# Three output projections, each in one stage with the layer norm that follows it

## The reference, cut to what matters

```
x = x + attn(norm(x));   attn ends in  out @ w_proj + b_proj + 2 * (out @ la @ lb)     (16 heads, causal)
x = x + xattn(norm(x));  xattn ends in out @ Wo + bo        (8 heads of 64, so out has 512 channels)
x = x + routed(norm(x)); routed ends in O @ Wo + bo         (4 of 16 heads of 64, chosen from the mean of norm(x))
x = x + attn2(norm(x)) ...
norm(x) = (x - mean) / sqrt(var + 1e-5), over the 256 channels, without gain or bias
```

## Time and profile before

| what | value |
|---|---|
| median of 3 runs | 2760.14 us (2759.46 to 2770.24) |
| the profiled execution's own time | 2762.19 us |
| its span | 2760.6 us |
| instructions | 39000 |
| TensorE's granted clock, mean | 0.838 of full speed |
| TensorE, VectorE, ScalarE, GpSimd busy | 73%, 60%, 38%, 31% of the span |

### The profile page before, as it was taken

The page is one execution under the profiler, slowest core; times in us unless marked ns, Lnnn a source line. Parts: engine busy times, 40 slices in busy tenths (PEclk is TensorE's granted clock), DMA queues, the critical chain, the costliest instruction groups (busy, mean ns, idle before and its releaser), DMA issues. The chain is left out here.

```text
span 2760.6 us, 39000 instructions
## 1 busy us (share of the span) xinstructions
PE 2008.9 (73%) x14317; PEld 1040.1 (38%) x14317; DVE 1660.4 (60%) x3077; ACT 1039.0 (38%) x1801; POOL 868.2 (31%) x1042
## 2 busy tenths in 40 slices
PE   7688887887479967899999723445828693269991
PEld 4233335324222234233333312232413473158991
DVE  4667643584358855778888259986674306445442
ACT  4377772241114423677777321112200312243330
POOL 3122220352224422585664002331451000422234
PEclk9699987898689988899999955556969895579996
DMA  5100000000100003000000320000200100432113
GB/s 185 45 19 25 22 9 26 1 1 11 28 1 1 1 18 126 28 31 29 33 28 23 111 68 1 2 2 21 73 28 30 36 1 5 167 135 78 47 51 99
DMA packets 79688, 113.44 MB, mean 41 GB/s; under 512 B 17861, under 2 KB 57809, under 8 KB 78481
## 3 DMA queue, kind: packets, MB, share of 16 engines
q1 hardware_dynamic: 70913, 99.04, 10.8%
q0 software_dynamic: 3664, 9.32, 1.2%
q10 hardware_dynamic: 4928, 2.62, 0.3%
HBM read 78.65 MB, written 32.05 MB: 40 GB/s over the span
## 5 line engine op out<-in xcount | busy, mean ns | idle before, releaser
L1181 DVE TENSOR_REDUCE a_mx<-a_SM 128x2 f32<-128x1024 f32 x256 | 299.7, 1216 | 66.5 <-PE a_SM L1054 66.1
L1164 ACT ACTIVATE a_P<-a_ST 128x512 f32<-128x512 f32 x512 | 292.9, 598 | 106.2 <-PE a_ST L1080 105.0
L876 ACT ACTIVATE a_P<-a_ST,a_scale 128x512 f32<-128x512 f32 (+3 forms) x384 | 206.7, 589 | 86.8 <-PE a_ST L788 85.2
L891 DVE TENSOR_REDUCE a_mx<-a_SM 128x2 f32<-128x1024 f32 (+1 forms) x192 | 176.2, 951 | 68.5 <-PE a_SM L753 37.7
L1080 PE MATMUL a_ST<-a_Q,a_K 98*128 98x512 bf16 (+1 forms) x512 | 187.3, 392 | 23.1 <-DMA a_Q<-a_MS 13.7
L1099 PE MATMUL a_OP<-a_P,a_V 128*32 128x256 f32 (+1 forms) x1792 | 157.9, 424 | 4.1 <-ACT a_P L1164 0.7
L723 POOL TENSOR_SCALAR_AFFINE_SELECT a_P<-a_P 128x128 f32<-128x128 f32 (+1 forms) x256 | 77.5, 307 | 245.5 <-ACT a_P L876 244.3
L3188 DVE TENSOR_TENSOR experts_hl<-work 128x512 bf16<-128x512 f32 x92 | 83.8, 969 | 89.5 <-POOL work L3038 89.5
L788 PE MATMUL a_ST<-a_Q,a_K 50*128 50x512 bf16 (+3 forms) x384 | 119.2, 359 | 24.8 <-ACT a_P L876 24.3
L3038 POOL CAST work<-work 128x512 bf16<-128x512 f32 x92 | 73.6, 840 | 200.6 <-PE experts_py L3122 186.3
L1080 PEld LDWEIGHTS a_ST<-a_Q,a_K 98*128 98x128 bf16 (+1 forms) x512 | 48.9, 101 | 180.3 <-issue 94.6
(11 more groups left out here) (545 smaller groups left out, 4814.9 us busy)
## 6 DMA issues: line engine op xcount, KB each, us to landing
work<-L_ffn_W SPq DMA_DIRECT2D x16, 1024.0 KB, 5.8
conv_tab<-dft_tables SPq DMA_DIRECT2D x8, 1024.0 KB, 5.0
bias_hankel<-bias_rows SPq DMA_DIRECT2D x16, 448.0 KB, 5.7
a_K<-a_k_parts SPq DMA_DIRECT2D x96, 64.0 KB
a_Q<-a_q_parts SPq DMA_DIRECT2D x96, 64.0 KB
expert_rows<-zeros SPq DMA_DIRECT2D x1, 5888.0 KB, 22.9
experts_xs<-expert_rows SPq DMA_DIRECT2D x23, 256.0 KB, 3.0
expert_results<-params SPq DMA_DIRECT2D x23, 256.0 KB, 2.1
```

Of the source, the lines that this page charges most:

```text
L876: act.activation(Pr[:, s % 2, u, j, c0:N], ST[:, u, c0:N], ACT.Exp, scale=kscale[:, 0:1]).then_inc(exp_done, 1)
L891: dve.tensor_reduce(mx[:, g % 2, qt, k0 // N, :], SM[:, c % 2, :, 0:kn], AX.X, ALU.max).then_inc(mx_read, 1)
L1164: act.activation(Pr[:, s % 2, u, j, :], ST[:, (4 * s + x) % 2, :], ACT.Exp, scale=scale).then_inc(exp_done, 1)
L1181: dve.tensor_reduce(mx[:, g % 2, qt, k0 // N, :], SM[:, c % 2, :, :], AX.X, ALU.max).then_inc(mx_read, 1)
```

## The change

`project` takes loaded weights instead of loading them, and contains the layer norm of its own result. Its transposes, those of the input in the first stage too, use two PSUM banks instead of four.

- VectorE, after adding pair j, takes the statistics of pair j-1. After the pairs 2, 4 and 6 it also merges the statistics of one group of four tiles, after the pairs 3, 5 and 7 it inverts the root of one group and forms a shift; the last group comes behind the last pair.
- ScalarE takes the square root of each group and normalises tiles 0 to 13 with an activation that has scale and bias; VectorE normalises tiles 14 and 15. ScalarE copies the turned groups 0 to 2 out, VectorE the last.
- TensorE turns group 0 after pair 4, group 1 after pair 6, groups 2 and 3 after pair 7. The work that stood beside the norms is put after pair 1. `ContextWork` now turns both its inputs through one pair of banks, so TensorE waits for ScalarE's copy between them.
- The four transfers for the first projection are issued at the end of `n0_fetch`, the two for the second in `n1_fetch`, which runs in the first joint stage, and the two for the third in `m0_load`, on SyncE, behind its wait for the chosen weights. The weights of `a1_qkv` are loaded in the third joint stage.
- The stages `n1`, `n2`, `n3` disappear. Semaphores are still cleared at `choose`: 111 have been used there.

```diff
-def project(nc, K, name, Y, width, weight, bias, lora=None, turned=False):
+def project(nc, K, name, Y, width, Wt, brow, loaded, lora=None, turned=False, dst=None, dstT=None, fetch=None, beside=None):
+
 
     WC = width // P
+    GROUPS, BANKS = TT // 4, 2
     with Stage(nc, name) as st:
         YT = Y if turned else st.sb("YT", [P, WC, B * S])
-        Wt = st.sb("W", [P, WC, D])
-        brow = st.sb("bias", [P, D])
-        pm, pw = st.ps("mm", [P, 3, 2, D]), st.ps("w", [P, D])
-        loaded, wmm, wready, biased = st.sem("loaded"), st.sem("wmm"), st.sem("wready"), st.sem("biased")
-        mm, added = st.sem("mm"), st.sem("added")
+        nx = st.sb("nx", [P, TT, D]) if dst is None else dst
+        stats, aggr, std = st.sb("stats", [P, TT, 6]), st.sb("aggr", [P, TT, 2]), st.sb("std", [P, TT])
+        rstd, shift = st.sb("rstd", [P, TT]), st.sb("shift", [P, TT])
+        pm, pt = st.ps("mm", [P, 3, 2, D]), st.ps("turned", [P, BANKS, N])
+        wmm, wready, biased, mm, added = (st.sem(x) for x in ("wmm", "wready", "biased", "mm", "added"))
+        stats_done, aggr_done, std_done, inverted, ready = (st.sem(x) for x in (
+            "stats_done", "aggr_done", "std_done", "inverted", "ready"))
+        normed, normed_v, turns, moved, moved_v = (st.sem(x) for x in ("normed", "normed_v", "turns", "moved", "moved_v"))
         if lora is not None:
-            la, lb, laT = st.sb("la", [P, DC, HD]), st.sb("lb", [HD, D]), st.sb("laT", [HD, D])
-        nload = 2 + (2 if lora is not None else 0)
+            la, lb = lora
+            laT, pw = st.sb("laT", [HD, D]), st.ps("w", [P, D])
+        side = None if beside is None else beside(st)
+        first = [] if turned else [(g, c) for g in range(GROUPS) for c in range(WC)]
+        begun = len(first)
         with st.block() as block:
-            if not turned:
-                turn_t, turn_s, moved = transposer(st, Y, YT, width, K.ident, lambda e, t: None)
-                turns = TT // 4 * WC
-
             @block.sync
             def _(sp):
-                sp.dma_start(Wt[:], weight.rearrange("(c p) n -> p c n", p=P)).then_inc(loaded, 16)
-                sp.dma_start(brow[:], row(bias)).then_inc(loaded, 16)
-                if lora is not None:
-                    sp.dma_start(la[:], lora[0].rearrange("(c p) n -> p c n", p=P)).then_inc(loaded, 16)
-                    sp.dma_start(lb[:], lora[1]).then_inc(loaded, 16)
+                if fetch is not None:
+                    fetch(sp)
+                if side is not None:
+                    side.on_sync(sp)
 
             @block.tensor
             def _(pe):
-                pe.wait_ge(loaded, 16 * nload)
+                def turn(n, src, g, c):
+                    if n >= BANKS:
+                        pe.wait_ge(moved, n - BANKS + 1)
+                    for k in range(4):
+                        last = pe.transpose(pt[:, n % BANKS, k * P:(k + 1) * P], src[:, 4 * g + k, c * P:(c + 1) * P], K.ident[:])
+                    last.then_inc(turns, 1)
+
+                def turn_normed(g):
+                    pe.wait_ge(normed, min(4 * g + 4, TT - 2))
+                    if g == GROUPS - 1:
+                        pe.wait_ge(normed_v, 2)
+                    for c in range(DC):
+                        turn(begun + g * DC + c, nx, g, c)
+
+                pe.wait_ge(*loaded)
                 if lora is not None:
                     for c in range(DC):
                         last = pe.transpose(pw[0:HD, c * P:(c + 1) * P], la[:, c, :], K.ident[:])
@@ -1256,9 +1273,10 @@
                     for c in range(DC):
                         pe.wait_ge(wready, c + 1)
                         pe.matmul(pw[:], laT[:, c * P:(c + 1) * P], lb[:], start=True, stop=True).then_inc(wmm, 1)
-                if not turned:
-                    turn_t(pe)
-                    pe.wait_ge(moved, turns)
+                for n, (g, c) in enumerate(first):
+                    turn(n, Y, g, c)
+                if first:
+                    pe.wait_ge(moved, begun)
                 if lora is not None:
                     pe.wait_ge(wready, 1 + DC)
                 for j in range(TT // 2):
@@ -1270,18 +1288,78 @@
                             last = pe.matmul(pm[:, j % 3, k, :], YT[:, c, t * P:(t + 1) * P], Wt[:, c, :],
                                              start=c == 0, stop=c == WC - 1)
                     last.then_inc(mm, 1)
+                    if j == 1 and side is not None:
+                        side.on_tensor(pe)
+                    if j >= 4 and j % 2 == 0:
+                        turn_normed(j // 2 - 2)
+                for g in range(GROUPS - 2, GROUPS):
+                    turn_normed(g)
 
             @block.scalar
             def _(act):
+                def move(n, g, c, to):
+                    act.wait_ge(turns, n + 1)
+                    act.copy(to[:, c, g * N:(g + 1) * N], pt[:, n % BANKS, :]).then_inc(moved, 1)
+
+                def normalise(g, count):
+                    act.wait_ge(ready, g + 1)
+                    for t in range(4 * g, 4 * g + count):
+                        act.activation(nx[:, t, :], K.X[:, t, :], ACT.Identity, bias=shift[:, t:t + 1],
+                                       scale=rstd[:, t:t + 1]).then_inc(normed, 1)
+
+                def root(g):
+                    ts = slice(4 * g, 4 * g + 4)
+                    act.wait_ge(aggr_done, 4 * g + 4)
+                    act.activation(std[:, ts], aggr[:, ts, 1], ACT.Sqrt, bias=K.eps[:, 0:1]).then_inc(std_done, 1)
+
                 if lora is not None:
                     act.wait_ge(wmm, 1)
                     act.mul(laT[:], pw[0:HD, :], 2.0).then_inc(wready, 1)
-                if not turned:
-                    turn_s(act)
+                for n, (g, c) in enumerate(first):
+                    move(n, g, c, YT)
+                if side is not None:
+                    side.on_scalar(act)
+                for g in range(GROUPS - 1):
+                    root(g)
+                    normalise(g, 4)
+                    if g < GROUPS - 2:
+                        for c in range(DC):
+                            move(begun + g * DC + c, g, c, dstT)
+                root(GROUPS - 1)
+                normalise(GROUPS - 1, 2)
+                for c in range(DC):
+                    move(begun + (GROUPS - 2) * DC + c, GROUPS - 2, c, dstT)
+
+            @block.gpsimd
+            def _(pool):
+                if side is not None:
+                    side.on_gpsimd(pool)
 
             @block.vector
             def _(dve):
-                dve.wait_ge(loaded, 16 * nload)
+                def add(j):
+                    x = K.X[:, 2 * j:2 * j + 2, :]
+                    dve.wait_ge(mm, j + 1)
+                    dve.tensor_tensor(x, x, pm[:, j % 3, :, :], ALU.add).then_inc(added, 1)
+
+                def measure(j):
+                    dve.wait_ge(added, j + 1)
+                    for t in (2 * j, 2 * j + 1):
+                        dve.bn_stats(stats[:, t, :], K.X[:, t, :]).then_inc(stats_done, 1)
+
+                def gather(g):
+                    dve.wait_ge(stats_done, 4 * g + 4)
+                    for t in range(4 * g, 4 * g + 4):
+                        dve.bn_aggr(aggr[:, t, :], stats[:, t, :]).then_inc(aggr_done, 1)
+
+                def invert(g):
+                    ts = slice(4 * g, 4 * g + 4)
+                    dve.wait_ge(std_done, g + 1)
+                    dve.reciprocal(rstd[:, ts], std[:, ts]).then_inc(inverted, 1)
+                    dve.wait_ge(inverted, g + 1)
+                    dve.scalar_tensor_tensor(shift[:, ts], aggr[:, ts, 0], -1.0, rstd[:, ts], ALU.mult, ALU.mult).then_inc(ready, 1)
+
+                dve.wait_ge(*loaded)
                 if lora is not None:
                     for c in range(DC):
                         dve.wait_ge(wmm, c + 2)
@@ -1290,9 +1368,23 @@
                                   ALU.add).then_inc(biased, 1)
                 dve.wait_ge(biased, 1)
                 for j in range(TT // 2):
-                    dve.wait_ge(mm, j + 1)
-                    dve.tensor_tensor(K.X[:, 2 * j:2 * j + 2, :], K.X[:, 2 * j:2 * j + 2, :], pm[:, j % 3, :, :],
-                                      ALU.add).then_inc(added, 1)
+                    add(j)
+                    if j:
+                        measure(j - 1)
+                    if j >= 2 and j % 2 == 0:
+                        gather(j // 2 - 1)
+                    if j >= 3 and j % 2:
+                        invert(j // 2 - 1)
+                measure(TT // 2 - 1)
+                gather(GROUPS - 1)
+                invert(GROUPS - 1)
+                for t in range(TT - 2, TT):
+                    dve.tensor_scalar(nx[:, t, :], K.X[:, t, :], aggr[:, t, 0:1], rstd[:, t:t + 1],
+                                      ALU.subtract, ALU.mult).then_inc(normed_v, 1)
+                for c in range(DC):
+                    n = begun + (GROUPS - 1) * DC + c
```

(40 more changed lines are left out.)

14 lines of the change are left out of this document (6 added, 8 removed).

## The result

The changed kernel takes 2755.57 us (median of 20 runs, 2741.30 to 2767.89), the kernel before on the same chip 2763.67 (20 runs, 2755.69 to 2774.92): ratio 0.9969, 95% interval [0.9955, 0.9983], which is 8.6 us less (the medians differ by 8.1). Measured twice more, beside later experiments (e12 and e13), the ratio was 0.9955 [0.9942, 0.9968] and 0.9963 [0.9946, 0.9981]. The mean is 0.9962, **-10.4 us**, where the prediction had -13.6. The predicted time was 2746.5 us, in a range of 2737 to 2755. Of the 9.1 us between 2746.5 and 2755.57, 3.5 are the kernel before: its median was 2763.67 over 20 runs, and the prediction started from the 2760.14 of three. In all that follows, medians and ratios leave out two single executions, 2901.20 us in e2 and 2884.96 in e3, whose granted clock was 0.75 where all others had 0.83 to 0.85.

A forecast was written before the change was run, and what follows sets the result against it. At the three places of the change a chain of waits, not an engine, was taken as the limit. The terms, led by -15.1 and -26.0 against added costs, summed to -13.6 us; from 2760.14 that gave 2746.5 us, range 2737 to 2755.

The forecast's parts named there:

- The heads: Starts of the three projections: with weights already there, work begins 4.1, 5.8 and 5.2 us sooner; together -15.1 us.
- the joints: Three projections with norms, from the stage before's end to the next stage's first work: predicted -0.8, -10.25 and -7.3 us.
- A: First of the three projections, between causal and cross attention: start 4.1 us sooner, end-of-products wait 9.2 instead of 16.3 us.
- The tails: From each projection's last product to the next stage: 9.2, 10.7, 9.2 us instead of 16.3, 18.35, 20.4; together -26.0.
- the gaps: TensorE's waits before turning groups 0 and 1: 2.2 us each in first and third projections, 0.45 in the second; +9.7.
- the queue of `n0`: Four more transfers on SyncE at the end of `n0`, 0.49 us each, delay `a0_qkv`: +1.9 us.
- the clock term: TensorE's low clock: two waits at 1.5 us, cold starts behind first and third projections 1.2 each; +5.4, bounds 2.4 and 9.6.
- The third rival: Every wait between the products lowers TensorE's clock, 1.8 us each: 2750.7 us; chance 0.15.
- The fourth rival: VectorE or ScalarE doesn't keep up in first and third projections, so waits grow: 2750.5 or 2753.4 us; chance 0.15.
- The fifth: TensorE stays at 1.2 GHz from pair 2 in first and third projections: 2764 us, 2790 with the second; chance 0.05.
- The first: Waits between products don't lower the clock: 2743.5 us, 2738 if the end stays at the high clock too; chance 0.25.
- The `m0_load` term: Two more transfers behind SyncE's wait in `m0_load`: between nothing and 1.0 us, taken as +0.5.

The follow-up runs named there:

- e12: The changed kernel, unaltered, measured again on another chip: 2748.24 us, ratio 0.9955 to the kernel before.
- e13: The changed kernel, unaltered, measured a third time: 2751.59 us, ratio 0.9963 to the kernel before.
- e2: The kernel before with only four transfers added at the end of `n0_fetch`, into buffers nobody reads: 2764.83 us, ratio 1.0006.
- e3: The changed kernel with groups 0 and 1 turned behind pairs 5 and 7 instead of 4 and 6: 2741.61 us, ratio 0.9929 to the kernel before.
- e7: The kernel before with the three projections' weights loaded ahead, norms still stages of their own: 2748.27 us, ratio 0.9949.
- e4: The changed kernel with each inverse and shift ahead of the addition of pairs 3, 5 and 7: 2738.54 us, ratio 0.9923 to the kernel before.

## Why the prediction was right or wrong

**Right.** The heads: -15.1 predicted, -14.1 timed and -13.3 in the joints. In A 1.4 us of the 4.1 comes back, since more of the transposes of the input then run at the low clock (6.51 us in e7 in place of 5.15). The tails, the gaps and the queue of `n0` came out within 0.2 us each. The three joints together: -18.35 predicted, -18.5 measured. That this is so close is partly luck: the 3.0 us that the clock term had put behind the gaps were 1.7 there, and 1.4 came at A's transposes, where it had none. The third rival (every gap lowers the clock) fell: of the twelve gaps in A and C of the three executions nine did not. The rule that the prediction names from the Trainium skill (TensorE: Matmul & The Clock Gate, "HAM oscillation — how this bites in real kernels"), that TensorE work cut up by waits can lose the full clock at every wait, is borne out here as something that can happen, behind three of these twelve gaps; the example on that page has longer waits than 2.10 us, so it gave no ground to expect a fall behind each of them. The fourth rival fell too: the gaps in A and C were 2.10 and no more. The fifth did not come. The first, which has no fall behind a gap, is what e12's profile shows, but the cold starts behind the tail that it leaves out came there too.

**Wrong: the size of one term, TensorE's clock, +5.4.** This is the step that failed. It held "Of the four I count two, at 1.5 each", 3.0, and one in four came, at about 1.7 us: 1.7. It held "1.2 in A and in C" for the next stage's cold start; measured 2.1 and 2.0. And it left out two places where earlier or later work meets the low clock: the transposes of A, +1.4, and the first attention's products, +2.1 (slow in most profiles without the four loads too, so not surely the change's in full). That makes 1.7 + 4.1 + 1.4 + 2.1 = 9.3 in place of 5.4, within the term's own bounds (2.4 to 9.6). The `m0_load` term, +0.5, was -0.3, and "two banks +0.2" is at most that. So the sum came out 3 us short of the -13.6.

**Wrong: that 2760.14 is what the kernel before takes.** Five series of 17 to 20 runs, the one beside the result among them, had 2759.86 to 2763.67. A median of three runs, where the single ones of a series range over 12 to 20 us, can move the forecast by as much as the error of the sum. Here it moved it by 3.5 us, and without that the median would have lain inside a range of the same width: 2755.57 is only 0.57 above its end. The error of the sum is 3.2 of the 9.1 us, and the remaining 2.4 are the spread between the three measurements of the change, of which this one showed the smallest gain.

**Missed.** The sentence "Group 0 can't be inverted before pair 3 is added, since VectorE works in that order" priced the gap right (2.2, measured 2.10) and took the order as given. e4 shows the price of that order: 10.8 us (6 to 15 by its interval).

Open: why the causal attention differs by up to 19 us between executions (325.8 to 345.1), how much of that a change before it can steer, and what decides behind which gap the clock falls.

## What to carry to other kernels

When a chain over three engines goes round between products, ask of each short step on it (here 0.34 us of inverse and shift) what longer work stands in front of it in its engine's order; moved ahead, it was worth more here (14.3 us of the joints) than choosing a faster engine for the long step (6.4). Measure the parts of a change alone: here the early loads were all of its gain, and the fusion paid for itself only once the order was mended. Price the granted clock wherever a stage's start moves or a run of dense work in front of it goes, not only where a gap appears, and don't read 10 us from one execution.
